# A four-block transformer on one core: local-attention values sent through DRAM, parts of its FFN and table loads moved, and two attentions with their heads' scores put side by side

## The chip, the cores and the metric

The program runs on one core of a Trainium2 chip, in float32. The metric is the device time of one execution in microseconds (us). The engines of a core work side by side, each on its own list of instructions in order, and wait for each other on semaphores: TensorE (PE) multiplies matrices into banks of PSUM; VectorE (DVE), ScalarE (ACT) and GpSimd (POOL) work on rows of 128 partitions; SyncE (SP) issues DMAs.

## What is computed

16 sequences of 256 tokens with 128 channels pass through four blocks, each an attention and a feed-forward part, all with a residual. Block 0 has plain attention (16 heads of 64), block 1 the same with a causal mask, and the second part of block 2 is a stack of six local transformer layers, the largest part of the time:

```python
# block 0 and 1, per sequence and head (block 1: causal mask)
probs = softmax(einsum('bid,bjd->bij', q, k) * 64**-0.5, axis=2)
out = einsum('bij,bjd->bid', probs, v)

# block 2, six times, over 16 heads of 64, windows of 32 tokens
def shift_tokens(t):                   # half of the channels come one token late
    a, s = split(t, 2, -1)
    s = pad(s, ((0, 0), (1, 0), (0, 0)))[:, :-1]
    return concatenate([a, s], -1)

def attn_layer(x, Wqkv, qs, ksc, Wo):
    q, k, v = split(x @ Wqkv, 3, -1)   # into heads
    q, k = l2norm(q) * qs, l2norm(k) * ksc
    q, k = rotary(q), rotary(k)
    # a window's queries look at its own keys and the window's before
    sim = where(mask, -max, einsum('bhwie,bhwje->bhwij', bq, look(bk)) * 8.0)
    out = einsum('bhwij,bhwje->bhwie', softmax(sim, -1), look(bv))
    return out @ Wo

def ffn_layer(x, g, bln, W1, b1, W2, b2):
    xn = layernorm(x) * g + bln
    a, gate = split(xn @ W1 + b1, 2, -1)
    return a * gelu(gate) @ W2 + b2
```

In each local layer both parts get token-shifted input and are added to the residual.

## The kernel before

The kernel writes out, by hand, a list of instructions for each engine and the semaphores between them. No scheduler reorders it: what stands first on an engine runs first.

**`attention`** serves blocks 0 (its names begin with `a0`) and 1 (`a1`). Two heads of 64 are one group; 8 groups of 16 sequences are 128 items. In an item TensorE turns (transposes) the probabilities of an earlier item (`turn`, L494), makes the scores of the next (`scores`, L486), multiplies turned probabilities with values (`weigh`, L505 and L506), projects queries, keys and values for a later one (L465, L472) and projects the output (L514). DVE takes the maximum of the scores (L716; L713 with the mask) and scales the exponentials (L722, L726); ACT makes the exponentials (L605), and copies out of PSUM (L568, L569, L575, L593, L611). The queries and keys of head 0 lie in partitions 0 to 63, of head 1 in 64 to 127. With `by_turns`, which holds for two heads without rotation, the order is turn of head 0, scores of head 0, turn of head 1, scores of head 1.

**`local_layers`** goes through 96 iterations `g`, 6 layers of 16 sequences. An iteration has two halves, `o` = 0 and 1, of 8 heads each; `h = 2g + o` counts halves. A half works on what three steps of the pipeline need: it projects queries and keys for half `h + 2` (`project_rows`, L1019), takes scores of half `h` from 128 small matmuls (`scores`, L1049), projects values (`project_v`, L1025), turns and weighs the probabilities (`turn_probs` L1061, `turn_qk` L1035, `weigh` L1075). DVE rotates queries and keys (L1297, L1301), masks scores and takes their maxima (`shift_scores`, L1330, L1334), sums exponentials (`invert_sums`, L1339, L1341); POOL subtracts the maximum (L951), divides by the sum (L957) and works on the rotation (L937, L944); ACT squares (L1198), copies and makes the exponentials (L1214).

The values of a half are needed in windows of 64 keys (a window and the one before), so each row is needed twice. Before, `x` has a pad of one window, POOL's `copy_window` (L970) writes the transposed input in overlapping windows into `x_windows`, and `project_v` projects each row twice (four matmuls of 512 columns, written as eight passes), with four moves of ACT (`move_v`, L1202).

The output projection (`output`, L1088) of an iteration adds to the residual the attention of the one before (`add_output`). The feed-forward part of an earlier sequence goes along: its rows are normalised (`row_stats` L1348 to L1353, `normalise_rows`), turned (`turn_normed`, L1095), multiplied with two matrices (`gates` and `ups`), the gates pass through Gelu on ACT (`open_gates`, L1237), DVE multiplies both (`hide_rows`, L1371), and TensorE projects down (`give`); DVE adds a bias and that result to the residual (`add_ffn`, L1384, L1388). Half of a row's channels comes one token late: SP brings the shifted rows (`shift`, L881 and L882; 127 partitions, and one row more) and stages the next input (`stage_x`, L876). ACT loads a table (ACT_TABLE_LOAD) when it goes from some functions to others: in the trace a load stands in front of an iteration's first squares (L1198) and one in front of the Gelu (L1237). Behind the Gelu it calls Square on one element (`warm`, L1281).

Where a step waits is written in its function: `output` and `give` wait for `g_freed`, `hide_rows` for `g_filled`, `weigh` for turned probabilities.

Of the kernel before, what the change touches and what calls it, by code (L numbers as in the profile page):

```python
# [286 lines left out]
def attention(core, name, w_dram, src_t, res, groups, heads, causal=False, window=False, scale=None,  # L287
# [39 lines left out]
    with ExitStack() as ctx:  # L327
# [50 lines left out]
        with nc.Block() as block:  # L378
# [64 lines left out]
            def _(pe):  # L443
# [87 lines left out]
                by_turns = heads == 2 and not rotary  # L531

                def item(quad, p, buffers, b, gp):
# [248 lines left out]
def local_layers(core, name, t, y, base, w, fw, gains):  # L782
# [13 lines left out]

    t_filled = core.sems(name, "t_filled0", "t_filled1")
    t_freed = core.sems(name, "t_freed0", "t_freed1")
    (cleared, staged, x_moved, window_ready, f_filled, f_freed, g_filled, g_freed, rows_filled, squared, sin_done, reduced,
     summed, newton, rot_ready) = core.sems(  # L800
        name, "cleared", "staged", "x_moved", "window_ready", "f_filled", "f_freed", "g_filled", "g_freed", "rows_filled",
# [6 lines left out]
     fw_loaded, scales_loaded, tables_ready) = core.sems(  # L808
        name, "shift_loaded", "stats_done", "stats_ready", "var_ready", "rstd_ready", "normed", "bias_added",
        "ffn_added", "w_loaded", "fw_loaded", "scales_loaded", "tables_ready")  # L810

    with ExitStack() as ctx:
# [4 lines left out]
        x, x_windows = sb("x", [P, W + SEQ]), sb("x_windows", [P, 4, 2, 2, W])  # L817
# [27 lines left out]
        def t_fill(h):  # L845

            return 5 * h + 4
# [5 lines left out]
        def hidden_fill(g):  # L853

            return f_fill(g) + (2 if not isinstance(g, int) or g < LAST else 1)
# [16 lines left out]
        with nc.Block() as block:  # L872
            @block.sync
            def _(sp):
# [14 lines left out]
                def iteration(g):  # L889
# [4 lines left out]
                    stage_x(g + 2)  # L894
                    sp.wait_ge(normed, g + 1)
# [3 lines left out]
                    shift((g + NB - 1) & (NB - 1))  # L899

                def load_layer(L):

                    sp.wait_ge(ffn_added, NB * L + 19)
                    sp.sem_inc(begun, 1)
                    sp.dma_start(fw[:], t["f2"][bass.ds(L + 1, 1), :, :].rearrange("a p n -> p (a n)")).then_inc(fw_loaded, DMA)
# [7 lines left out]

                load_scales(0)
                stage_x(0)
                shift(NB - 2)
                sp.wait_ge(f_filled, 1)
                stage_x(1)
                with sp.Fori(0, DEPTH) as L:
                    with sp.Fori(0, 3) as m:  # L920
                        iteration(NB * L + m)
                    load_layer(L)
# [10 lines left out]
            def _(pool):  # L933
# [47 lines left out]
                def iteration(g, last=False):  # L981
                    for o in range(2):
# [5 lines left out]
                        if o == 0:  # L988
                            deviations(g)
# [1502 lines left out]
```

## Time and profile before

| | before |
|---|---|
| median of 3 runs | 7244.83 us (7240.41 to 7246.15) |
| profiled execution | 7247.5 us |
| its span | 7245.8 us |
| mean granted TensorE clock | 0.977 |
| PE busy | 6522.4 us (90%) |
| DVE busy | 4927.7 us (68%) |
| ACT busy | 4182.4 us (58%) |
| POOL busy | 2901.3 us (40%) |

The span is the time from the profile's first to its last record. The busy time of an engine is a sum over stages which differ. The plain attention of block 0 lies between 74 and 857 us, that of block 1 between 1081 and 1765, the local layers between 2241 and 6346.

### The profile page before, as it was taken

How to read it: one execution, taken by the hardware profiler on the slowest of the kernel's cores; microseconds unless marked ns; L12 is line 12 of the kernel's file. 1: busy time of each engine (PE TensorE's matmuls, PEld its weight loads, DVE VectorE, ACT ScalarE, POOL GpSimd, SP SyncE). 2: the span in 40 equal slices, each digit the busy share in tenths (PEclk: the TensorE clock that was granted, in tenths of full speed). 3: DMA queues.
4: the chain of work that ended last, by engine and by line, in shares of the span. 5: the costliest groups of instructions: out<-in, count | busy, mean ns of one | idle time of the engine just before them, and what ended most of it. 6: DMA issues, size and time to landing. Idle time of an engine off the chain costs nothing. (4 is left out here: it accounts for less than half of the span.)

```text
span 7245.8 us, 217809 instructions
## 1 busy us (share of the span) xinstructions
PE 6522.4 (90%) x79314; PEld 4468.9 (62%) x79314; DVE 4927.7 (68%) x14182; ACT 4182.4 (58%) x10030; POOL 2901.3 (40%) x2911
## 2 busy tenths in 40 slices
PE   7999979999988888888888888888888888879998
PEld 5777657776655565555555556555555555557676
DVE  4555535555657777777777777777777777668378
ACT  4666637776224655656655665565665566446355
POOL 0000010000004666666666666666666666530030
PEclk9999989999989999999999999999999999979999
DMA  1000000000000000000000000000000000010210
GB/s 34 24 25 25 23 27 29 28 28 22 10 33 20 23 4 5 23 4 5 5 23 5 4 5 22 5 5 4 23 5 4 23 4 5 5 37 16 81 38 24
DMA packets 131939, 133.17 MB, mean 18 GB/s; under 512 B 40302, under 2 KB 121982, under 8 KB 130814
## 3 DMA queue, kind: packets, MB, share of 16 engines
q1 hardware_dynamic: 115454, 103.45, 4.4%
q0 software_dynamic: 7936, 24.28, 1.1%
q10 hardware_dynamic: 8448, 4.20, 0.2%
q8 instruction: 51, 0.84, 0.0%
q14 instruction: 50, 0.41, 0.0%
HBM read 55.48 MB, written 10.49 MB: 9 GB/s over the span
## 5 line engine op out<-in xcount | busy, mean ns | idle before, releaser
L937 POOL TENSOR_TENSOR l_rot<-l_rot,l_by_sin 128x512 f32<-128x512 f32 x768 | 961.1, 1272 | 438.6 <-DVE l_by_sin L1301 424.5
L944 POOL TENSOR_TENSOR l_rot<-l_rot,l_norms 128x512 f32<-128x512 f32 x768 | 793.7, 1064 | 485.0 <-DVE l_norms L1322 485.0
L1019 PE MATMUL bank<-w_w,l_x 128*128 (+1 forms) x1536 | 802.0, 631 | 133.8 <-DVE l_by_sin L1301 126.3
L1198 ACT ACTIVATE l_squares<-bank 128x512 f32<-128x512 f32 x768 | 447.5, 596 | 518.9 <-DVE l_square_sums L1306 491.8
L1025 PE MATMUL bank<-w_w,l_x_windows 128*128 (+1 forms) x1536 | 721.0, 602 | 0.0
L1297 DVE TENSOR_TENSOR l_rot<-bank,l_cos 128x512 f32<-128x512 f32 x768 | 519.2, 676 | 295.7 <-ACT l_squares L1198 294.4
L486 PE MATMUL bank<-a_qk 64*128 64x256 f32 (+2 forms) x2660 | 679.5, 381 | 6.1 <-DVE a_qk L668 3.5
L402 POOL DMA_DIRECT2D a_w<-in_a x23 | 13.0, 565 | 1554.2 <-PE bank L514 1431.0
L593 ACT ACTIVATE a_probs_t<-bank 128x512 f32<-128x512 f32 (+1 forms) x656 | 355.9, 554 | 353.7 <-PE bank L494 353.7
L1219 ACT ACTIVATE l_probs_t<-bank 128x512 f32<-128x512 f32 x384 | 208.7, 595 | 598.2 <-PE bank L1061 598.2
L1035 PE MATMUL bank<-ident,l_rot 128*128 128x128 f32 x3072 | 476.4, 283 | 74.3 <-ACT l_probs_t L1219 48.0
L1025 PEld LDWEIGHTS bank<-w_w,l_x_windows 128*128 128x128 f32 x1536 | 260.0, 189 | 429.1 <-issue 429.0
L1301 DVE TENSOR_TENSOR l_by_sin<-bank,l_sin 128x512 f32<-128x512 f32 x768 | 521.8, 679 | 0.9 <-POOL l_rot L937 0.9
L1019 PEld LDWEIGHTS bank<-w_w,l_x 128*128 128x128 f32 x1536 | 246.0, 189 | 443.9 <-issue 438.7
L951 POOL TENSOR_TENSOR l_probs<-l_probs,l_best 128x512 f32<-128x512 f32 x384 | 400.2, 1042 | 282.4 <-DVE l_best L1334 282.4
L1202 ACT ACTIVATE l_v<-bank 128x512 f32<-128x512 f32 x768 | 451.3, 588 | 103.6 <-PE bank L1025 103.6
L1208 ACT ACTIVATE l_qk<-bank 128x512 f32<-128x512 f32 x768 | 450.0, 597 | 90.5 <-PE bank L1035 87.2
L486 PEld LDWEIGHTS bank<-a_qk 64*128 64x128 f32 (+1 forms) x2660 | 410.6, 188 | 135.2 <-issue 91.7
L1306 DVE TENSOR_REDUCE l_square_sums<-l_squares 128x8 f32<-128x512 f32 x768 | 486.4, 674 | 0.0
L716 DVE TENSOR_REDUCE a_neg_max<-bank 128x1 f32<-128x256 f32 x780 | 294.6, 419 | 270.8 <-PE bank L486 262.5
L1035 PEld LDWEIGHTS bank<-ident,l_rot 128*128 128x128 f32 x3072 | 322.2, 140 | 229.4 <-ACT l_probs_t L1219 92.7
L957 POOL TENSOR_TENSOR l_probs<-l_probs,l_inverse 128x512 f32<-128x512 f32 x384 | 400.2, 1042 | 126.6 <-DVE l_inverse L1341 126.5
(265 smaller groups left out, 14415.8 us busy)
## 6 DMA issues: line engine op xcount, KB each, us to landing
a_x<-normed_t SPq DMA_DIRECT2D x320, 128.0 KB, 2.0
l_stage_rows<-inner SPq DMA_DIRECT2D x98, 128.0 KB, 2.1
w_w<-in_w SPq DMA_DIRECT2D x6, 2048.0 KB, 9.5
l_shifted_half<-inner SPq DMA_DIRECT2D x98, 63.5 KB
f_w<-in_f SPq DMA_DIRECT2D x9, 514.5 KB, 3.2
a_w<-in_a POOLq DMA_DIRECT2D x18, 256.0 KB, 2.9
f_w<-in_f POOLq DMA_DIRECT2D x9, 512.0 KB, 4.4
c_x<-normed_t SPq DMA_DIRECT2D x36, 128.0 KB, 2.0
```

The lines of the kernel that those rows point to most:

```text
L486: last = nc.tensor.matmul(bank[:, t * SEQ + k0:t * SEQ + k1], queries, qk[p % 2][rows_of_head, keys_at + k0:keys_at + k1], start=True, sto ...
L937: nc.gpsimd.tensor_tensor(rot[s][n][:], rot[s][n][:], by_sin[n % 2][:], ALU.add).then_inc(summed, 1)
L944: nc.gpsimd.tensor_tensor(mine, mine, along(norms[s][:, 8 * n:8 * n + 8], HD), ALU.mult)\
L1019: nc.tensor.matmul(rows_p[i][:], x[:, W + i * P:W + (i + 1) * P], layer_w(layer, quad * QUAD, QUAD), start=True, stop=True).then_inc(rows_ ...
L1025: nc.tensor.matmul(t_p[j % 2][:], x_windows[:, j].rearrange("p t s c -> p (t s c)"), layer_w(layer, wv_at + o * QUAD, QUAD), start=True, s ...
L1035: last = nc.tensor.transpose(t_p[i][:, tile_of(n)], rot[s][2 * a + i][:, tile_of(n)], core.ident[:])
L1198: nc.scalar.activation(squares[i][:], rows_p[i][:], ACT.Square).then_inc(squared, 1)
L1202: nc.scalar.activation(v[:, j, o * QUAD:(o + 1) * QUAD], t_p[j % 2][:], ACT.Copy).then_inc(t_freed[j % 2], 1)
L1208: nc.scalar.activation(qk[o][:, :, 2 * a:2 * a + 2, W + i * P:W + (i + 1) * P], t_p[i][:].rearrange("p (n h s) -> p n h s", n=2, h=2), ACT ...
L1297: nc.vector.tensor_tensor(rot[s][2 * a + i][:], rows_p[i][:], cos[:, i, :], ALU.mult)
L1301: nc.vector.tensor_tensor(dst, src[:, :, ::-1, :], table, ALU.mult).then_inc(sin_done, 1)
L1306: nc.vector.tensor_reduce(square_sums[:, 8 * n:8 * n + 8], squares[i][:].rearrange("p (h d) -> p h d", d=HD), AX, ALU.add)\
```

## The change

In **`attention`** `by_turns` goes. TensorE turns both heads, then makes the scores of both, then weighs.

In **`local_layers`**:

- `x` has no pad, and `x_windows` and `copy_window` go. `project_v` projects each row once, two matmuls for a half in place of four; two moves of ACT put them in `v_rows`. SP stores them to DRAM (`store_v`, 512 KB), behind a window of zeros, and after the weighing of half `h` loads them back into `v` for half `h + 2` as overlapping windows (`load_v`, four DMAs of 256 KB). `weigh` waits for `v_loaded`.
- The FFN: `ups` comes ahead of the scores of the first half and `give` ahead of the scores of the second. On DVE `normalise_rows` begins the iteration, `hide_rows` follows the masked scores of the first half, `add_ffn` and `row_stats` of the next iteration follow those of the second, and `add_output` ends the first half. `fw` is loaded in parts (`gates_loaded`, `ups_loaded`).
- ACT calls Exp on one element (`warm`) at the start of an iteration, and Gelu on one element behind the exponentials of the second half. The first square of an iteration goes to the end of the one before.
- On SP, an iteration is: `stage_x`, the store and the loads of values of the first half, the wait for `normed` and `added`, the `shift`, then the store and the loads of values of the second half.

```diff
@@ attention, item
-                            if by_turns:
-                                scores(k + 1, p + 1, j)
-                        if not by_turns:
-                            for j in pass_heads:
-                                scores(k + 1, p + 1, j)
+                        for j in pass_heads:
+                            scores(k + 1, p + 1, j)
@@ local_layers, SP
+                def store_v(u, o, fill):
...
+                    sp.dma_start(v_dram[o][W:, :].rearrange("(i p) n -> p i n", p=P), v_rows[:]).then_inc(v_stored, DMA)
+                def load_v(u, o):
+                    sp.wait_ge(v_stored, (u + 1) * DMA)
...
+                    for i in range(2):
+                        for s in range(2):
+                            at = i * P + s * W
+                            sp.dma_start(v[HD * i + W * s:HD * i + W * (s + 1), :, o * QUAD:(o + 1) * QUAD],
+                                         v_dram[o][at:at + P, :].rearrange("(j c) n -> c j n", c=W)).then_inc(v_loaded[o], DMA)
+                def send_v(g, o):
+                    h = 2 * g + o
+                    sp.wait_ge(v_loaded[o], (g + 1) * 4 * DMA)
...
+                    store_v(h + 2, o, t_fill(h))
+                    sp.wait_ge(heads_filled, 4 * h + 4)
...
+                    load_v(h + 2, o)
                 def iteration(g, L=None, last=False):
...
                     stage_x(g + 2)
...
+                    if not last:
+                        send_v(g, 0)
                     sp.wait_ge(normed, g + 1)
                     sp.wait_ge(added, g + 2)
                     shift((g + NB - 1) & (NB - 1))
...
+                    if not last:
+                        send_v(g, 1)
@@ PE
                 def project_v(o, fill, layer):
-                    for j in range(4):
...
-                        nc.tensor.matmul(t_p[j % 2][:], x_windows[:, j].rearrange("p t s c -> p (t s c)"),
+                    for i in range(2):
+                        reached(pe, t_freed[i], fill)
+                        nc.tensor.matmul(t_p[i][:], x[:, tile_of(i)], layer_w(layer, wv_at + o * QUAD, QUAD), start=True,
+                                         stop=True).then_inc(t_filled[i], 2)
@@ weigh
+                    pe.wait_ge(v_loaded[o], ((h >> 1) + 1) * 4 * DMA)
@@ iteration, PE
                             project_rows(h + 2, o, 0, (g + 1) >> 4)
+                        if o == 0:
+                            ups(g)
+                        else:
+                            give(g)
                         scores(h, o)
                         if not last:
                             project_rows(h + 2, o, 1, (g + 1) >> 4)
+                            project_v(o, fill, (g + 1) >> 4)
                         if o == 0:
-                            project_v(1, fill, g >> 4)
                             output(g)
-                            give(g)
...
                         weigh(h, o, turned)
-                        if o == 1:
-                            ups(g)
@@ iteration, ACT
+                    nc.scalar.activation(warm[:], core.ones[:, 0:1], ACT.Exp)
...
+                            exps(h, 1)
+                            nc.scalar.activation(warm[:], core.ones[:, 0:1], ACT.Gelu)
                         move_probs(turned)
...
-                            nc.scalar.activation(warm[:], core.ones[:, 0:1], ACT.Square)
                         move_heads(h, o)
+                    if not last and squared_next:
+                        square(2 * g + 4, 0)
@@ iteration, DVE
+                    normalise_rows(g)
...
                         shift_scores(h, 0)
                         shift_scores(h, 1)
+                        if o == 0:
+                            hide_rows(g)
+                        else:
+                            add_ffn(g)
+                            row_stats(g + 1)
                         invert_sums(h, 0)
                         invert_sums(h, 1)
-                        if o == 0:
-                            row_stats(g)
...
                         if o == 0:
                             add_output(g)
-                            add_ffn(g)
-                        else:
-                            hide_rows(g)
```

TensorE, the beginning of an item in block 0's attention, before; `a_probs_0` and `a_probs_1` are the two heads (the rows name instructions of the program, not times):

```order
L494 MATMUL bank<-ident,a_probs_0 128x128 x4
L478 REGISTER_ALU
L480 ISA
L486 MATMUL bank<-a_qk 128x256 x2
L492 REGISTER_ALU
L494 MATMUL bank<-ident,a_probs_1 128x128 x4
L486 MATMUL bank<-a_qk 128x256 x2
L505 MATMUL bank<-a_probs_t,a_v 64x256
L506 MATMUL bank<-a_probs_t,a_v 64x256
L505 MATMUL bank<-a_probs_t,a_v 64x256
L506 MATMUL bank<-a_probs_t,a_v 64x256
```

and after the change:

```order
L494 MATMUL bank<-ident,a_probs_0 128x128 x4
L492 REGISTER_ALU
L494 MATMUL bank<-ident,a_probs_1 128x128 x4
L478 REGISTER_ALU
L480 ISA
L486 MATMUL bank<-a_qk 128x256 x4
L505 MATMUL bank<-a_probs_t,a_v 64x256
L506 MATMUL bank<-a_probs_t,a_v 64x256
L505 MATMUL bank<-a_probs_t,a_v 64x256
L506 MATMUL bank<-a_probs_t,a_v 64x256
```

The scores of both heads now stand next to each other, behind both turns.

TensorE, the second half of a local iteration, from its scores to the values, before:

```order
L1049 MATMUL bank<-l_qk 32x64 x64
L843 REGISTER_ALU
L1019 ISA
L1019 MATMUL bank<-w_w,l_x 128x512
L843 REGISTER_ALU
L1019 MATMUL bank<-w_w,l_x 128x512
L1025 ISA
L1025 MATMUL bank<-w_w,l_x_windows 128x512 x2
L843 REGISTER_ALU
L1025 MATMUL bank<-w_w,l_x_windows 128x512 x2
```

and now, from its first row projection on; `w_f, l_hidden` is `give`, and L1066, L1072 and L1095 are the former L1019, L1025 and L1049:

```order
L1066 MATMUL bank<-w_w,l_x 128x512 x2
L1174 MATMUL bank<-w_f,l_hidden 128x128 x6
L1088 ISA
L1095 MATMUL bank<-l_qk 32x64 x64
L841 REGISTER_ALU
L1066 ISA
L1066 MATMUL bank<-w_w,l_x 128x512
L841 REGISTER_ALU
L1066 MATMUL bank<-w_w,l_x 128x512
L1072 ISA
L1072 MATMUL bank<-w_w,l_x 128x512 x2
```

The down projection came in ahead of the scores, and half of the values' projections are gone.

DVE, the second half of a local iteration, from the first masking to the sums, before:

```order
L1330 TENSOR_TENSOR l_probs<-bank,masks 128x512
L1333 ISA
L1334 TENSOR_REDUCE l_best<-l_probs 128x8
L1330 TENSOR_TENSOR l_probs<-bank,masks 128x512
L1333 REGISTER_ALU
L1334 TENSOR_REDUCE l_best<-l_probs 128x8
L1339 TENSOR_REDUCE l_sums<-l_probs 128x8
L1341 RECIPROCAL l_inverse<-l_sums 128x8
L1339 TENSOR_REDUCE l_sums<-l_probs 128x8
L1341 RECIPROCAL l_inverse<-l_sums 128x8
```

and now, from behind the last maximum (L1405, formerly L1334) to the first sum (L1410, formerly L1339):

```order
L1456 ISA
L1456 TENSOR_TENSOR inner<-inner,w_f 128x256
L1460 TENSOR_TENSOR inner<-inner,bank 128x256
L1416 ISA
L1419 BN_STATS l_stats<-l_shifted_half 128x6
L1420 BN_STATS l_stats<-inner 128x6
L1419 BN_STATS l_stats<-l_shifted_half 128x6
L1420 ISA
L1420 BN_STATS l_stats<-inner 128x6
L1421 ISA
L1424 BN_AGGR l_mean_var<-l_stats 128x2 x2
L1410 TENSOR_REDUCE l_sums<-l_probs 128x8
```

`add_ffn` (L1456, L1460) and the statistics (L1419 to L1424) moved between the maximum and the sum.

## Rows read from the trace of the kernel before

**Rows 1.** Busy time by stretch: us, PE, PEld, DVE, ACT, POOL; PEclk, DMA, GB/s.

```profile
74.00:857.00 783.00, 779.40 (x4560) 558.10 (x4561) 420.69 (x1394) 535.37 (x1778) 4.30 (x8) 1.00 0.07 24
1081.00:1765.00 684.00, 679.94 (x4372) 497.78 (x4370) 388.64 (x2192) 506.72 (x1807) 4.29 (x8) 0.99 0.08 28
2247.00:6307.00 4060.00, 3595.54 (x62587) 2366.20 (x62587) 3082.48 (x7497) 2433.98 (x4318) 2704.27 (x2688) 1.00 0.03 10
```

**Rows 2.** Timeline, first attention: start us, us, engine, line, operation, idle before.

```profile
500.85 0.38 ACT L611 ACTIVATE a_heads_t<-bank 128x256 f32<-128x256 f32 x1 [0.59 <-PE bank L506]
501.13 0.47 ACT L605 ACTIVATE a_probs<-bank,a_neg_max 128x256 f32<-128x256 f32 x1
...
502.02 0.39 ACT L568 ACTIVATE a_qk<-bank 128x256 f32<-128x256 f32 x1
...
502.37 0.62 DVE L726 TENSOR_SCALAR a_probs<-a_probs,a_inverse 128x256 f32<-128x256 f32 x2
...
504.17 0.66 PE L494 MATMUL bank<-ident,a_probs 128*128 128x128 f32 x4
...
504.75 1.13 PE L486 MATMUL bank<-a_qk 64*128 64x256 f32 x4
...
505.92 0.76 DVE L716 TENSOR_REDUCE a_neg_max<-bank 128x1 f32<-128x256 f32 x2 [0.89 <-PE bank L486]
```

**Rows 3.** Timeline of the second attention, same columns.

```profile
1502.71 0.55 PE L494 MATMUL bank<-ident,a_probs 128*128 128x128 f32 x3
...
1503.18 0.92 PE L486 MATMUL bank<-a_qk 64*128 64x128 f32 x4
...
1504.70 0.08 DVE L713 DVE_READ_ACCUMULATOR2_ANT a_neg_max<- 128x1 f32 x1
```

**Rows 4.** Timeline of one iteration of the local layers, same columns.

```profile
4000.34 1.98 PE L1019 MATMUL bank<-w_w,l_x 128*128 x4
...
4002.25 1.48 PE L1049 MATMUL bank<-l_qk 64*32 64x64 f32 x128
...
4010.63 3.73 PE L1088 MATMUL bank<-w_w,l_heads_t 128*128 x32
...
4015.55 1.04 PE L1061 MATMUL bank<-ident,l_probs 128*128 128x128 f32 x8
...
4021.59 1.98 PE L1019 MATMUL bank<-w_w,l_x 128*128 x4
...
4022.77 2.65 SPq L882 DMA_DIRECT2D l_shifted_half<-inner  x1
...
4029.08 0.69 DVE L1334 TENSOR_REDUCE l_best<-l_probs 128x8 f32<-128x512 f32 x1
...
4030.27 0.69 DVE L1339 TENSOR_REDUCE l_sums<-l_probs 128x8 f32<-128x512 f32 x1 [0.50 <-ACT l_probs L1214]
...
4032.59 1.04 POOL L957 TENSOR_TENSOR l_probs<-l_probs,l_inverse 128x512 f32<-128x512 f32 x1 [0.28 <-DVE l_inverse L1341]
...
4042.07 1.27 DVE L1371 SCALAR_TENSOR_TENSOR l_hidden<-bank,w_f,l_gate 128x256 f32<-128x256 f32 x3 [3.50 <-PE bank L1102]
...
4042.45 1.98 PE L1019 MATMUL bank<-w_w,l_x 128*128 x4
```

**Rows 5.** Timeline at the end of the local layers, same columns.

```profile
6317.98 0.42 DVE L1384 TENSOR_TENSOR inner<-inner,w_f 128x256 f32<-128x256 f32 x1
...
6319.50 0.28 DVE L1353 BATCH_NORM_AGGREGATE l_mean_var<-l_stats 128x2 f32<-128x12 f32 x2
...
6321.88 0.75 SPq L881 DMA_DIRECT2D l_shifted_half<-inner  x1
...
6331.82 0.22 DVE L1348 BATCH_NORM_STATS2 l_stats<-l_shifted_half 128x6 f32<-128x64 f32 x1
```

**Rows 6.** DMA issues: queue, count, KB each, median us from issue to landing.

```profile
l_stage_rows<-inner SPq DMA_DIRECT2D x98, 128.0 KB, 2.1
w_w<-in_w SPq DMA_DIRECT2D x6, 2048.0 KB, 9.5
```

More of the change, by code:

```diff
@@ L912, in load_layer, with layer @@
                         .then_inc(w_loaded, DMA)
+                def layer(L):
+                    with sp.Fori(0, 2) as m:
+                        iteration(NB * L + m)
+                    iteration(NB * L + 2, L)
+                    load_layer(L)
                 load_scales(0)
                 stage_x(0)
+                sp.wait_ge(cleared, 2)
+                for o in range(2):
+                    sp.dma_start(v_dram[o][0:W, :], heads_t[0:W, 0:2, :].rearrange("p a n -> p (a n)")).then_inc(v_cleared, DMA)
+                sp.wait_ge(v_cleared, 2 * DMA)
                 shift(NB - 2)
@@ L918, in _ @@
                 stage_x(1)
[L919 to L922, printed above, removed]
+                for u in range(2):
+                    store_v(u, u, u)
+                    load_v(u, u)
+                with sp.Fori(0, DEPTH - 1) as L:
+                    layer(L)
                     with sp.Fori(3, NB) as m:
                         iteration(NB * L + m)
+                layer(DEPTH - 1)
+                with sp.Fori(NB * (DEPTH - 1) + 3, LAST) as g:
+                    iteration(g)
+                iteration(LAST, last=True)
                 sp.wait_ge(normed, LAST + 2)
@@ L1144, in iteration @@
                         fill, more = t_fill(h), o == 0 or not last
-                        turned = fill + 2 if more else fill
+                        turned = fill if last else fill + 1
                         if not last:
@@ L1178, in finish @@
                         gates(g)
-                        ups(g)
+                    ups(LAST + 3)
                     give(LAST + 3)
@@ L1248, in start, with iteration @@
                     square(0, 1)
-                    for j in range(4):
-                        move_v(0, j, 0)
+                    for i in range(2):
+                        move_v(0, i, 0)
                     square(1, 0)
                     square(1, 1)
+                    for i in range(2):
+                        move_v(1, i, 1)
                     move_qk(0, 2)
                     move_x(1, 1)
-                def iteration(g, last=False):
+                def iteration(g, last=False, squared_next=True):
+                    nc.scalar.activation(warm[:], core.ones[:, 0:1], ACT.Exp)
@@ L1257, in iteration @@
                     for o in range(2):
                         h = 2 * g + o
-                        fill, more = t_fill(h), o == 0 or not last
+                        fill = t_fill(h)
+                        turned = fill if last else fill + 1
                         if not last:
-                            square(h + 2, 0)
+                            if o == 1:
+                                square(h + 2, 0)
                             square(h + 2, 1)
-                        if more:
-                            move_v(1 - o, 0, fill)
-                            move_v(1 - o, 1, fill)
@@ L1277, in iteration @@
+                        move_probs(turned)
+                        if o == 0 or not last:
+                            move_qk(1 - o, turned + 1)
                         if o == 0:
@@ L1287, in finish @@
                         open_gates(g)
-                run(act, start, iteration, finish)
+                start()
+                square(2, 0)
+                with act.Fori(0, LAST - 1) as g:
+                    iteration(g)
+                iteration(LAST - 1, squared_next=False)
+                iteration(LAST, last=True)
+                finish()
             @block.vector
```

189 lines of the change are left out of this document (103 added, 86 removed).

## The prediction

> **What bounds the kernel now.** I read the busy time by stretch first. The stretch of the local layers has 4060 us (all but 45 of them), the first attention 783, the second 684 [rows 1], of a span of 7245.8; the change touches these three. In both attentions TensorE is busy over 99% of the stretch, in the local layers 3595.5 of 4060 (89%) with DVE at 76% and POOL at 67%. A busy TensorE need not be the bound: one item of the first attention takes 783/128 = 6.12 us, and to see what its next item waits for I then read the timeline. There the two heads follow each other: transposes of a head's probabilities, the next item's scores of the same head, then the other head; DVE's two maxima start 1.17 us behind the scores [rows 2]. Everything goes round in a loop, with TensorE filling it.
>
> For the local layers I took one iteration of the timeline [rows 4]: 4042.45 − 4000.34 = 42.11 us, in two halves whose projections start at 4000.34 and 4021.59, so 21.25 and 20.86. No engine fills a half. Each half is one chain: project rows, rotate and score, masked maximum (the second of a half ends 4029.08 + 0.69 = 4029.77, 8.18 behind the half's start), subtract and exponentiate, sum (starts 4030.27), divide (the last division ends 4033.63, 3.36 behind the sum), transpose, weigh, then the next half. Transposes to next half: 4015.55 to 4021.59 = 6.04. In the first half the chain is stretched by the values' projection (two of four in each half) and by the FFN, whose gates wait behind table loads; in the second by the up-projection, with `hide_rows` at its very end [rows 4] (its last two rows).
>
> **The attentions, part by part.** Both heads' transposes now come first, then both scores. The contraction of a head is 64 rows, and the two heads sit in different row halves. If they run together, TensorE does 1.13 us less in an item of the first attention. That they can: the 128 score matmuls of 64x32 tiles of the local layers take 1.48 us [rows 4], 11.6 ns each, whereas 4 of 64x128 over 256 columns take 1.13 [rows 2], so 64 columns cost 0.07 and 128 of them 9.0; four quarters of the columns alone would leave 2.3, so row halves overlap too. With less work than the loop is long, what then sets the item is the loop: second transpose to scores 504.75 − 504.17 = 0.58; scores to DVE 505.92 − 504.75 = 1.17; the first head's two maxima 0.76; a wait of 0.10; the first head's exponentials 502.02 − 501.13 = 0.89; the heads' copy between, 501.13 − 500.85 = 0.28; the second head's exponentials to the end of its scaling, 502.37 + 0.62 − 501.13 = 1.86; a wait of 0.06. Sum 5.70 [rows 2]. So 6.11 − 5.70 = 0.41 less, times 128 items: **−52**. The two waits are estimates, the smallest gaps between such neighbours. By TensorE alone it would be −1.13 x 128 = −145; if the heads' scores don't overlap, the maxima come 1.13 later in the loop, 6.8 in place of 6.11, +0.69 x 128 = +88.
>
> The Trainium skill, "TensorEngine Tiling (Array Packing)", section "Theoretical Speedup", gives up to 2x for a contraction of at most 64. By that sentence the whole 1.13 would be won; it speaks of the array, and is the rule behind rival B.
>
> The second attention is causal and its scores are shorter: 0.92 us a head [rows 3]. Its loop: transposes 1502.71 to the end of the maxima 1504.78 = 2.07, then 0.10 + 0.89 + 0.28 + 1.86 + 0.06 as above, 5.26 in all, against 684/128 = 5.34 now: 0.08 x 128 = **−10**. By TensorE alone −0.92 x 128 = −118; without overlap 6.16, +105.
>
> **The local layers, part by part.** (1) Values: the projection falls from 4 matmuls of a half to 2, the moves of ACT likewise, POOL's window copies go; a store of 512 KB and four loads of 256 KB come for each half through DRAM. TensorE loses about what four passes of the row projection take, 1.98 us a half [rows 4], work that is off the chain except where it holds the next waiting instruction. A loaded value is used a whole iteration later: 38 us as summed below, less its issues, against 9.5 us for a 2 MB load [rows 6], so I cost the loads at nothing; they would show from a latency of that length. (2) Table loads: two of an iteration, in front of the squares and of the gates; now ACT makes them where it waits for TensorE. They have no term of their own, since I build the new halves from links that hold none. (3) The FFN: ups ahead of the scores of the first half, `hide_rows` (1.27 [rows 4]) between the maxima and the sums there; give ahead of the scores of the second, `add_ffn` and the statistics between maxima and sums there. From the end of the stage, where nothing else runs, 6317.98 to 6319.50 + 0.28 is 1.80 for the latter [rows 5]; I take 2.0, an estimate, since ACT and POOL run beside it here. Neither hides fully behind ACT's exponentials, which they wait beside: the gap from maximum to sum is only 0.50 [rows 4].
>
> New first half: 8.18 + 1.27 = 9.45; 0.1 wait; the output projection ahead of the transposes holds TensorE about 3.6 (3.73 now [rows 4]), longer than the 3.36 of sums to division: 13.2; then 6.04 to the next half: 19.25. New second half: 8.18 + 2.0 = 10.2; 3.36; 0.1; and 6.04 less an estimated 0.4, since half of its transposes (1.04 for eight [rows 4]) are done before the last division, less 0.3, without the normalised rows' transpose: 5.35: 19.0. Together 38.25 against 42.11, −3.86 in each of 95 repeats: **−367**. Of the bounds: nothing gained if the FFN's 3.07 in the chain replace as much of what they remove (rival D); and TensorE's work, 3595.54/4060 x 42.11 = 37.3 less 2 x 1.98 = 33.3 in an iteration, as the floor, −8.8 x 95 = −836, which the chains above don't let it reach. The clock was granted in full in these stretches (1.00, 0.99, 1.00: 2.4 GHz [rows 1]), with TensorE at 89% in the last; 33.3 of 38.25 is 87%, so I change nothing for it.
>
> (4) The shift of rows, needed by the statistics, is issued by SP after the values' store and loads of the first half. SP waits there for the weighing, about +19.25; four issues at 0.45 to 0.75 (the shift's own first issue [rows 5]; 0.45 is my estimate for them), then the shift's two, 0.75 and 2.65 [rows 4, 5], end at +24.5 to 25.7, and it lands 2.1 later (a 128 KB transfer's [rows 6]): +26.6 to 27.8. The statistics want it behind the maxima and two additions of 0.42 [rows 5]: 19.25 + 8.18 + 0.84 = 28.3. So it is in time by 0.5 to 1.7 us, and I cost it at nothing. The upper end is in the end of the stage: issued from 6321.88, used at 6331.82 [rows 5], 9.9 us; with that it lands 2.8 too late.
>
> The Trainium skill, "DMA: Bandwidth & Descriptors", section "Why a DMA increments its semaphore by 16 and not by 1", says that a transfer of 127 partitions runs on a single DMA engine; the shift has 127 rows, so the megabyte of values issued ahead of it would keep that engine's queue. No row here splits transfers by engine; it speaks for rivals A and A'.
>
> Sum against the profiled execution's 7247.5: −52 − 10 − 367 gives 6818; this execution is 2.7 above the median of the runs, so **6816**.
>
> **Rivals.** *A: the shift is late* by up to the 2.8 us above: at 2 us in each of 95 iterations, +190: 7006; at 2.8, 7082. For it: SP now has five more issues and three waits ahead of the shift. Against: the slack of 0.5 to 1.7 us, if it lands as small transfers do. *A', on the slow side: the shift late behind the megabyte of values.* With 4.7 us of a load ahead of it (half of 9.5 for half the bytes [rows 6]) on top of 2.8, 7.5 late: 6816 + 712 = 7530. It decides from about 4.5 us late, where 95 x 4.5 = 428 eats the gain. Against: the page's DMA share of the stretch is 0.03 [rows 1], so the queues are empty but for this. *B: TensorE stays the bound in both attentions* and the loops overlap better than I add them: −145 − 118 in place of −62: 6615. Against: DVE's wait behind the scores is in the loop. *C: the heads' scores don't overlap*, +88 + 105 in place of −62: 7071. Against: the 1.48 us of the local scores. *D: the local layers stay at 42.1*, because the FFN's links now lie in the chain: 7247.5 − 2.7 − 62 = 7183. For it: DVE goes to 84% busy in the new iteration (32.0 of 38.25) and its queue is in order.
>
> **Numbers.** Forecast 0.62, A 0.15, A' 0.07, B 0.05, C 0.06, D 0.05. The forecast's own range is 6740 to 6900: each half's sum may be off by 0.4 us, which is 76 over 95 iterations. The range that takes in A and C: 6720 to 7082; outside are B, D, A' with 0.17. This kernel's measurement can tell 0.2% from no change. Faster: all but A' and the lateness between A and A', 0.91; same 0.01; slower 0.08.
>
> **What will show it.** The period between two iterations' first projections, 38.25; the halves 19.25 and 19.0; an item of 5.70 in the first attention and 5.26 in the second, with TensorE's share there falling below 95% and DVE named as the releaser of the exponentials. The statistics' first instruction without a wait for a DMA behind the second half's maxima: with such a wait it is A or A', and its length says which. Scores of both heads in one 1.13 us group, else C. No table load with a TensorE wait behind it. I am wrong if the halves are not shortened in the places named: the sum depends on the two links into which the FFN went being 1.27 and 2.0, and on TensorE's 3.6 of output standing beside the division.

## The result, and the profile after

The changed kernel takes 7376.39 us (median of 4 runs, 7374.58 to 7378.20) against 7242.62 before: ratio 1.0184, 95% interval 1.0172 to 1.0197. It is 1.8% slower; I had forecast 6816 us.

| | before | after |
|---|---|---|
| span of the profiled execution | 7245.8 us | 7376.5 us |
| mean granted TensorE clock | 0.977 | 0.947 |
| PE busy | 6522.4 us (90%) | 6135.0 us (83%) |
| DVE busy | 4927.7 us (68%) | 5156.6 us (70%) |
| ACT busy | 4182.4 us (58%) | 3982.4 us (54%) |
| POOL busy | 2901.3 us (40%) | 2823.1 us (38%) |

Busy time by stretch, after, the same stretches and columns as [rows 1] (each kernel is at another place of its work in the last of them):

```profile
74.00:857.00 783.00, 706.09 (x4763) 511.56 (x4764) 441.73 (x1437) 548.20 (x1842) 4.38 (x8) 0.99 0.08 27
1081.00:1765.00 684.00, 611.38 (x4374) 445.96 (x4373) 400.08 (x2159) 471.06 (x1694) 3.76 (x7) 1.00 0.08 27
2247.00:6307.00 4060.00, 3266.68 (x58959) 2343.10 (x58960) 3164.66 (x7157) 2157.45 (x3846) 2505.48 (x2382) 0.95 0.31 80
```

The loss lies in the third row: TensorE's granted clock (the share of its full clock that the chip lets it have), 1.00 before, is 0.95 in the local layers, and DVE is busier although the stretch now holds fewer iterations (92 outputs of 32 passes; before, 96).

The two attentions did what was forecast. Timeline of the first one, with [rows 2] before (start us, us, engine, line, operation):

```profile
505.64 0.66 PE L494 MATMUL bank<-ident,a_probs 128*128 128x128 f32 x4 [0.52 <-DVE a_probs L722]
...
506.22 1.14 PE L486 MATMUL bank<-a_qk 64*128 64x256 f32 x8
...
511.29 0.66 PE L494 MATMUL bank<-ident,a_probs 128*128 128x128 f32 x4 [0.52 <-DVE a_probs L722]
```

Both heads' scores, now eight passes in one group, take 1.14 us; one head's four took 1.13. An item takes 511.29 − 505.64 = 5.65 us (forecast 5.70, before 6.11). In the second attention, with [rows 3] before:

```profile
1502.50 0.55 PE L494 MATMUL bank<-ident,a_probs 128*128 128x128 f32 x3 [0.59 <-DVE a_probs L722]
...
1502.98 0.93 PE L486 MATMUL bank<-a_qk 64*128 64x128 f32 x8
...
1507.58 0.55 PE L494 MATMUL bank<-ident,a_probs 128*128 128x128 f32 x3 [0.58 <-DVE a_probs L722]
```

7.58 − 2.50 = 5.08 us an item (forecast 5.26, before 5.34).

Now one iteration of the local layers, with [rows 4] before; L1066 is the row projection (L1019), L1135 the output (L1088), L1432 `normalise_rows`, L1419 the first of the statistics:

```profile
4010.36 1.98 PE L1066 MATMUL bank<-w_w,l_x 128*128 x4 [0.59 <-issue]
...
4012.12 1.08 DVE L1432 TENSOR_SCALAR l_normed_rows<-inner,l_mean_var,l_rstd 128x64 f32 x1
...
4018.95 0.69 DVE L1405 TENSOR_REDUCE l_best<-l_probs 128x8 f32<-128x512 f32 x1
...
4019.56 1.26 DVE L1443 SCALAR_TENSOR_TENSOR l_hidden<-bank,w_f,l_gate 128x256 f32<-128x256 f32 x3
...
4021.30 5.46 PE L1135 MATMUL bank<-w_w,l_heads_t 128*128 x32 [2.52 <-DVE l_hidden L1443]
...
4026.59 1.04 PE L1107 MATMUL bank<-ident,l_probs 128*128 128x128 f32 x8
...
4032.64 1.98 PE L1066 MATMUL bank<-w_w,l_x 128*128 x4
...
4035.30 0.78 SPq L887 DMA_DIRECT2D l_shifted_half<-inner  x1
...
4036.22 4.76 SPq L888 DMA_DIRECT2D l_shifted_half<-inner  x1
...
4043.57 0.23 DVE L1419 BATCH_NORM_STATS2 l_stats<-l_shifted_half 128x6 f32<-128x64 f32 x1 [1.96 <-DMA l_shifted_half<-inner]
...
4044.53 0.63 DVE L1410 TENSOR_REDUCE l_sums<-l_probs 128x8 f32<-128x512 f32 x1
```

and the projection that begins the next iteration:

```profile
4053.66 1.55 PE L1066 MATMUL bank<-w_w,l_x 128*128 x3 [0.62 <-issue]
```

The first half takes 4032.64 − 4010.36 = 22.28 us in place of the forecast 19.25, the second 4053.66 − 4032.64 = 21.02 in place of 19.0: 43.3 against 42.11 before. The mean is longer, 4060/92 = 44.1 us in the stretch of the local layers. Three things stand in these lines that the forecast didn't have: normalisations of 1.08 us at the start, an output projection of 5.46 us in place of 3.73, and 1.96 us in which DVE waits for the shift's DMA before the statistics.

The clock of TensorE in this iteration (us, busy time of PE, PEld, DVE, ACT, POOL, then PEclk, DMA share and GB/s):

```profile
4018.80:4021.30 2.50, 0.00 (x1) 0.01 (x1) 2.46 (x6) 1.62 (x3) 1.68 (x2) 1.00 0.00 0
4021.30:4023.00 1.70, 1.70 (x8) 1.70 (x9) 1.63 (x6) 0.61 (x2) 1.28 (x2) 0.52 0.05 17
4023.00:4025.00 2.00, 2.00 (x12) 2.00 (x12) 2.00 (x5) 0.00 (x0) 2.00 (x3) 0.56 0.66 248
4025.00:4026.80 1.80, 1.80 (x18) 1.80 (x18) 1.66 (x6) 0.00 (x0) 1.22 (x1) 1.00 0.00 0
4032.64:4053.66 21.02, 15.69 (x319) 10.81 (x313) 16.05 (x39) 12.82 (x24) 10.44 (x11) 1.00 0.31 78
```

TensorE waits 2.5 us for `hide_rows`; then, in the output, the granted clock is 0.52 and 0.56, the lower of its two levels (1.2 GHz in place of 2.4), and 1.00 again at the output's end. Over the whole run the output's passes are busy for 507.2 us, before the change for 364.2.

Groups of DVE's instructions in the stretch of the local layers (busy us, mean ns, idle time before and its releaser):

```profile
L1432 DVE TENSOR_SCALAR l_normed_rows<-inner,l_mean_var,l_rstd 128x64 f32 (+1 forms) x182 | 187.9, 1033 | 86.1 <-DVE l_norms L1393 79.1 <-issue 5.8 <-DVE l_sin L1465 1.0
L1432 DVE TENSOR_SCALAR l_normed_rows<-l_shifted_half,l_mean_var,l_rstd 128x64 f32<-128x64 f32 x182 | 135.1, 742 | 0.0
...
L1419 DVE BATCH_NORM_STATS2 l_stats<-l_shifted_half 128x6 f32<-128x64 f32 x184 | 40.1, 218 | 204.8 <-DMA l_shifted_half<-inner 204.8
```

The normalisations' means are 1033 and 742 ns; the statistics wait 204.8 us for the shift, 2.2 us an iteration.

### The profile page after: what moved, and what is told of

It reads as the page before. It is cut to its first block and busy times, and to the rows that moved or that the text cites. A ratio compares the mean times of both kernels' runs of the same rounds, so it can differ in the third digit from the quotient of the medians.

```text
span 7376.5 us, 217475 instructions
## 1 busy us (share of the span) xinstructions
PE 6135.0 (83%) x78552; PEld 4414.5 (60%) x78552; DVE 5156.6 (70%) x14186; ACT 3982.4 (54%) x9742; POOL 2823.1 (38%) x2719
## 5 line engine op out<-in xcount | busy, mean ns | idle before, releaser
L1066 PE MATMUL bank<-w_w,l_x 128*128 (+1 forms) x1536 | 784.8, 628 | 115.4 <-issue 57.4
L1135 PE MATMUL bank<-w_w,l_heads_t 128*128 (+1 forms) x3104 | 507.2, 340 | 236.4 <-DVE l_hidden L1443 236.4
L1135 PEld LDWEIGHTS bank<-w_w,l_heads_t 128*128 128x128 f32 x3104 | 489.2, 252 | 315.4 <-issue 315.4
L1081 PE MATMUL bank<-ident,l_rot 128*128 128x128 f32 x3072 | 513.0, 305 | 79.8 <-ACT l_probs_t L1272 46.2
L601 ACT ACTIVATE a_probs<-bank,a_neg_max 128x256 f32<-128x256 f32 x780 | 363.1, 476 | 271.1 <-DVE a_neg_max L712 271.1
L494 PE MATMUL bank<-ident,a_probs 128*128 128x128 f32 x2352 | 374.1, 282 | 148.8 <-DVE a_probs L722 148.8
L1081 PEld LDWEIGHTS bank<-ident,l_rot 128*128 128x128 f32 x3072 | 368.9, 154 | 206.8 <-issue 95.3
L1066 PEld LDWEIGHTS bank<-w_w,l_x 128*128 128x128 f32 x1536 | 254.8, 190 | 370.2 <-issue 364.9
L486 PE MATMUL bank<-a_qk 64*128 64x256 f32 (+2 forms) x2660 | 423.7, 383 | 4.4 <-DVE a_qk L664 3.5
## 6 DMA issues: line engine op xcount, KB each, us to landing
l_shifted_half<-inner SPq DMA_DIRECT2D x98, 63.5 KB
```

Of the source, the lines that this page charges most:

```text
L486: last = nc.tensor.matmul(bank[:, t * SEQ + k0:t * SEQ + k1], queries, qk[p % 2][rows_of_head, keys_at + k0:keys_at + k1], start=True, sto ...
L1066: nc.tensor.matmul(rows_p[i][:], x[:, tile_of(i)], layer_w(layer, quad * QUAD, QUAD), start=True, stop=True).then_inc(rows_filled, 1)
L1081: last = nc.tensor.transpose(t_p[i][:, tile_of(n)], rot[s][2 * a + i][:, tile_of(n)], core.ident[:])
L1135: last = nc.tensor.matmul(out_p[:, tile_of(i)], heads_t[:, pair, tile_of(i)], layer_w(layer, wo_at + pair * P, P), start=pair == 0, stop=p ...
```

## The experiments

Each time stands beside one of the kernel before from the same chip, as a ratio with its 95% interval. The first four runs change one thing of the changed kernel each.

**The shift ahead of the loads.** SP's iteration:

```diff
-    send_v(g, 0)             # store, wait for the weighing, load
+    save_v(g, 0)             # store
     sp.wait_ge(normed, g + 1)
     sp.wait_ge(added, g + 2)
     shift((g + NB - 1) & (NB - 1))
+    fetch_v(g, 0)            # wait for the weighing, load
```

> In the first half SP issues the shift of rows before it waits for the weighing and loads the values; all else as in the changed kernel. Theory (the shift is late because it comes behind the loads of values): the statistics no longer wait for a DMA (204.8 us of that wait in the stretch of the local layers, about 2.2 an iteration); the sums that follow wait next for ACT's second exponentials, so about 1.5 us of an iteration are won: 96 x 1.5 = 144 less than 7376, about 7232. Rival (the statistics are not on the chain, TensorE's output and its clock set the iteration): the wait goes and the time stays within 30 us of 7376.

Measured 7077.39 us (ratio to before 0.9773, 0.9757 to 0.9790): 299 less than the changed kernel, twice what the wait alone was to give. DVE's groups:

```profile
L1438 DVE TENSOR_SCALAR l_normed_rows<-inner,l_mean_var,l_rstd 128x64 f32 (+1 forms) x186 | 190.8, 1026 | 87.8 <-DVE l_norms L1399 80.8 <-issue 5.8 <-DVE l_sin L1471 1.2
...
L1425 DVE BATCH_NORM_STATS2 l_stats<-l_shifted_half 128x6 f32<-128x64 f32 x188 | 40.3, 214 | 0.0
```

No wait is left before the statistics (L1425), and the normalisations are as slow as ever. TensorE's clock changed as well. An output (first row) and the second half of an iteration:

```profile
4014.66:4018.30 3.64, 3.64 (x32) 3.64 (x33) 3.57 (x9) 0.61 (x2) 3.22 (x3) 1.00 0.38 144
4024.38:4043.55 19.17, 15.57 (x319) 10.78 (x313) 15.89 (x39) 12.85 (x25) 12.13 (x13) 1.00 0.33 85
```

Before this output, too, TensorE idled 2.52 us, yet it runs at 1.00. What differs is the second half, in which TensorE now idles 19.17 − 15.57 = 3.60 us; in the changed kernel, 21.02 − 15.69 = 5.33 us. In the stretch of the local layers an output (32 passes) takes 396.2/93.8 = 4.22 us in the mean here, 480.1/92 = 5.22 there, 96 x 1.0 less. This output is not all of them: of the run's 97, 26 still take over 4.4 us, in the changed kernel 84. The transposes of the rotated queries and keys (L1081 in the changed kernel) are busy for 457.9 us in place of 513.0 over the run. With the 205 of the wait these parts come to 356, more than the 299, so not all of them lie on the chain.

**The shift in two pieces.** SP's order as changed; 127 partitions become 112 and 15, and the statistics wait for one transfer more:

```diff
-    sp.dma_start(shifted_half[1:P], rows[0:P - 1])
+    sp.dma_start(shifted_half[1:113], rows[0:112])
+    sp.dma_start(shifted_half[113:P], rows[112:P - 1])
...
-    dve.wait_ge(shift_loaded, (g + 1) * 2 * DMA)
+    dve.wait_ge(shift_loaded, (g + 1) * 3 * DMA)
```

> Order of SP as in the changed kernel; only the shift's transfer of 127 partitions is issued as one of 112 and one of 15. Theory (the transfer of 127 partitions runs at 15 GB/s, as the trace shows behind the loads, because one DMA engine does it alone): the pieces land some 3 us sooner and the statistics don't wait: about 7232, as with the shift put first. Rival (it is late because it is issued late, or queues behind the loads whatever its shape): the wait shrinks by less than 0.5 us of 2.2, and the time by less than 40 us.

Measured 7072.09 us (0.9764, 0.9748 to 0.9781), the same as with the order changed. To see why, the DMA rate in the changed kernel, 40 slices of 0.4 us from 4030 us on:

```profile
DMA  0000000000889999999995100000010199930000
GB/s 0 0 0 0 0 0 0 0 0 0 164 307 353 225 195 179 241 282 215 210 179 89 10 15 16 15 15 16 15 16 16 47 379 374 389 133 0 0 0 0
```

The loads of values run at up to 353 GB/s from slice 10 on (counted from 0). When they are done, some 3.6 us follow (slices 22 to 30) at 15 to 16 GB/s, the first at 10, with under a tenth of the engines busy: I read that as the shift. Its 63.5 KB at this rate are 4.1 us. In the split kernel, slices of 0.4 us from 4021 us on, the two pieces with the us from issue to landing, and DVE's group:

```profile
GB/s 0 0 0 0 0 0 0 0 0 0 0 0 0 0 0 0 0 0 0 0 0 0 236 276 302 261 195 184 225 230 205 200 205 163 97 6 0 0 0 0
...
l_shifted_half<-inner SPq DMA_DIRECT2D x1, 56.0 KB, 4.6
l_shifted_half<-inner SPq DMA_DIRECT2D x1, 7.5 KB, 4.0
```

```profile
L1420 DVE BATCH_NORM_STATS2 l_stats<-l_shifted_half 128x6 f32<-128x64 f32 x188 | 40.3, 214 | 0.0
```

The slow tail is gone and the statistics don't wait. So the shape of the transfer made it late, not its place behind the loads alone: either change is enough. The Trainium skill, "DMA: Bandwidth & Descriptors", section "Why a DMA increments its semaphore by 16 and not by 1", states that a transfer of 127 partitions runs on one engine; by its rule for the number of engines one of 112 runs on sixteen. The 15 to 16 GB/s and their end in the split agree, though no row here splits transfers by engine.

**The normalisation at its old place.**

```diff
-    normalise_rows(g)        # DVE, start of the iteration
     for o in range(2):
...
             sum_squares(h + 2, 1)
+        if o == 0:
+            normalise_rows(g)
+        if not last:
             norm_factors(h + 2, o)
```

> DVE normalises the rows where the kernel before did, behind the second sums of squares of the first half, not at the start of the iteration. Theory (the four normalisations, 0.74 to 1.03 us each now and 0.36 to 0.38 before, hold up the rotation by 1.1 us at the start of an iteration while POOL works): the first maxima come 1.1 sooner after the half's projection, TensorE idles less before its output: 96 x 1.1 = 105 less at least, 7270, and down to 7130 if the clock no longer falls in the output. Rival (the instructions are slow wherever they stand, and come to the chain at the new place): mean durations stay over 0.7, time within 30 us of 7376.

Measured 7073.05 us (0.9766, 0.9749 to 0.9782), 303 less. DVE's groups, and an output of this kernel:

```profile
L1432 DVE TENSOR_SCALAR l_normed_rows<-inner,l_mean_var,l_rstd 128x64 f32 (+1 forms) x188 | 63.2, 336 | 0.0
L1432 DVE TENSOR_SCALAR l_normed_rows<-l_shifted_half,l_mean_var,l_rstd 128x64 f32<-128x64 f32 x188 | 56.9, 303 | 0.0
L1419 DVE BATCH_NORM_STATS2 l_stats<-l_shifted_half 128x6 f32<-128x64 f32 x188 | 41.0, 218 | 214.1 <-DMA l_shifted_half<-inner 214.1
```

```profile
4013.20 3.83 PE L1135 MATMUL bank<-w_w,l_heads_t 128*128 x32 [1.45 <-DVE l_hidden L1443]
```

The same instructions take 336 and 303 ns at the other place, TensorE waits 1.45 us in place of 2.52 before the output, and the output takes 3.83 (5 of the run's 97 take over 4.4). The wait for the shift (L1419) stays, 214.1 us, and the second half stays long.

**More work for TensorE.** In the first half each matmul of the values is made twice:

```diff
+    if twice:
+        nc.tensor.matmul(t_p[i][:], x[:, tile_of(i)], layer_w(...), start=True, stop=True)
     nc.tensor.matmul(t_p[i][:], x[:, tile_of(i)], layer_w(...), start=True, stop=True).then_inc(...)
```

> In the first half each matmul of the values is done twice (the same result), 1.9 us more work for TensorE in the time in which it idles 2.4 us for the hidden rows before its output. Theory (the clock falls to half behind that idle time, and makes the output 5.5 us in place of 3.7): with the idle time filled the output takes 3.7 again, and the kernel with more work is faster by up to 96 x 1.55 = 149, about 7230 to 7290. Rival (the clock falls for another reason, or the added work delays the chain): the output stays at 5.5 and the time is 7376 or longer, by up to 96 x 1.9 = 182.

Measured 7249.57 us (1.0010, 1.0001 to 1.0020): 127 less than the changed kernel, with more work. The last of the doubled projections, the output, and the transposes of the rotated queries and keys (L1084) in the second half of the same iteration:

```profile
4010.10 1.02 PE L1075 MATMUL bank<-w_w,l_x 128*128 x2
4011.93 3.83 PE L1138 MATMUL bank<-w_w,l_heads_t 128*128 x32 [0.80 <-DVE l_hidden L1446]
...
4037.32 3.74 PE L1084 MATMUL bank<-ident,l_rot 128*128 128x128 f32 x16
```

The idle time before the output is 0.80 us, and it takes 3.83; only one of the run's 97 outputs takes over 4.4. So the fall of the clock in the output comes from TensorE's idling, and without it the kernel is 127 us shorter, the added work included. But the clock still falls elsewhere: in the second half, where nothing was filled, the transposes take 3.74 us at a granted clock of 0.54 (the same sixteen passes take 2.62 in the first half), and the stretch of the local layers has 0.97, against 0.95 in the changed kernel. So the 127 us are not the price of the whole fall.

**Both orders together.** The edits of the first and the third experiment.

> Both orders together: SP issues the shift before it loads the values, and DVE normalises where the kernel before did. Theory (two separate delays, one in each half, each of which also let the clock fall in TensorE's output): the first half takes 19.56 as with the late normalisation alone, the second 19.17 as with the early shift alone, 38.7 us an iteration: about 7073 - 96 x 2.0 = 6880. Rival (each of the two changes alone had already won what there is, namely the clock, and a third link takes over): 7040 or more.

Measured 6850.83 us (0.9463, 0.9448 to 0.9479): 5.4% faster than before, 526 less than the changed kernel. Alone the two won 299 + 303 = 602, so 76 are counted twice, as is to be expected if each alone had already won back much of the clock. The local layers' row of the stretches, and an iteration:

```profile
2247.00:5900.00 3653.00, 3136.26 (x60725) 2231.55 (x60717) 2998.77 (x7320) 2204.09 (x3945) 2568.11 (x2440) 1.00 0.35 91
```

```profile
4091.96 1.98 PE L1072 MATMUL bank<-w_w,l_x 128*128 x4 [0.64 <-issue]
...
4101.79 3.83 PE L1141 MATMUL bank<-w_w,l_heads_t 128*128 x32 [1.42 <-DVE l_hidden L1449]
...
4111.51 1.98 PE L1072 MATMUL bank<-w_w,l_x 128*128 x4
...
4130.60 1.98 PE L1072 MATMUL bank<-w_w,l_x 128*128 x4 [0.59 <-issue]
```

The clock is 1.00, and 4 of the run's 97 outputs take over 4.4 us. The halves take 4111.51 − 4091.96 = 19.55 and 4130.60 − 4111.51 = 19.09 us, 38.64 together: the forecast had 19.25 and 19.0.

**Without the early table loads**, from the run with both orders:

```diff
-    nc.scalar.activation(warm[:], core.ones[:, 0:1], ACT.Exp)
...
-            nc.scalar.activation(warm[:], core.ones[:, 0:1], ACT.Gelu)
```

> As the run with both orders, without the two calls of ACT on one element that load the tables early. Theory (a table load in front of the first half's exponentials is on the chain, that in front of the Gelu beside TensorE's weighing): 96 x 1.28 = 123 more than with them, and 246 if both are on the chain. Rival (ACT waits there anyway, the loads hide): within 20 us of the run with both orders.

Measured 6871.57 us (0.9489, 0.9473 to 0.9505): 21 more, not the 123 to 246 of the theory. ACT's groups:

```profile
L1296 ACT ACT_TABLE_LOAD x94 | 120.6, 1283 | 1.7
L1255 ACT ACT_TABLE_LOAD x92 | 118.0, 1283 | 308.4 <-PE bank L1072 308.4
```

Both loads, 1283 ns each, are there in every iteration, one in front of the Gelu (L1296) and one of the squares (L1255). So the chain bears 21/96 = 0.2 us of their 2.57 us; the two calls are worth little. That doesn't hold for the place of the loads: this run keeps the first squares at the end of the iteration before, and the load of L1255 comes where ACT has waited for TensorE, 308.4 us in all. In the kernel before, it stood in front of the first squares:

```profile
4001.56 1.28 ACT L1198 ACT_TABLE_LOAD   x1 [1.39 <-PE bank L1019]
...
4003.48 0.69 DVE L1297 TENSOR_TENSOR l_rot<-bank,l_cos 128x512 f32<-128x512 f32 x1 [2.26 <-ACT l_squares L1198]
...
4023.46 0.69 DVE L1297 TENSOR_TENSOR l_rot<-bank,l_cos 128x512 f32<-128x512 f32 x1 [0.92 <-ACT l_squares L1198]
```

There the rotation begins 4003.48 − 4000.34 = 3.14 us behind the projection [rows 4], in the second half, without a load, 4023.46 − 4021.59 = 1.87. So that load lengthened the way to the rotation by 1.27 us. No run moves the squares back alone.

**The attentions alone**, in the kernel before:

```diff
-    by_turns = heads == 2 and not rotary
+    by_turns = False
```

> The kernel before with the one change to the two attentions: both heads turned, then both scored. Theory (the part is independent of the rest, an item of the first attention 5.65 in place of 6.11, of the second near 5.26): 128 x 0.46 + 128 x 0.08 = 69 less than before, about 7174. Rival (the gain in the attentions is given back in the stages that follow): within 0.2% of before.

Measured 7159.66 us (0.9884, 0.9868 to 0.9901), 83 less than before; I had 62 in the prediction. The items' 0.46 and 0.26 us by 128 give 92. So the part is independent of the rest, and worth a third more than I had added up.

**The normalisation in another form**, at the changed place:

```diff
-    tensor_scalar(normed_rows[...], rows, mean_var[:, i, 0:1], rstd[:, i:i + 1], ALU.subtract, ALU.mult)
+    scalar_tensor_tensor(normed_rows[...], rows, mean_var[:, i, 0:1], rstd[:, i:i + 1].to_broadcast([P, D // 2]), ALU.subtract, ALU.mult)
```

> As the changed kernel, the four normalisations at the start of an iteration, but each as a SCALAR_TENSOR_TENSOR with the factor as a second tensor of SBUF (broadcast over the row) in place of a TENSOR_SCALAR with two factors. Theory (a DVE instruction of this size is held up only in the TENSOR_SCALAR form, by POOL's instruction that runs beside it): 0.2 to 0.4 us each in place of 0.74 to 1.03, and the time falls as with the late normalisation, to 7073 or near. Rival 1 (with two operands from SBUF the other form is held up by POOL just as well, as the Trainium skill's page on SBUF has it for two-input instructions): 0.7 us or more each, time within 30 us of 7376. Rival 2 (it is the place at the start of the iteration, whatever the instructions last): they are short, and the time stays.

Measured 7380.72 us (1.0186, 1.0168 to 1.0204): rival 1. The timeline of POOL's four multiplications with the norms, and DVE's instructions beside them:

```profile
4012.77 4.12 POOL L1005 TENSOR_TENSOR l_rot<-l_rot,l_norms 128x512 f32<-128x512 f32 x4 [2.37 <-DVE l_norms L1393]
...
4013.70 0.28 DVE L1432 SCALAR_TENSOR_TENSOR l_normed_rows<-inner,l_mean_var,l_rstd 128x64 f32<-128x64 f32 x1 [1.01 <-DVE l_norms L1393]
4013.90 1.06 DVE L1432 SCALAR_TENSOR_TENSOR l_normed_rows<-l_shifted_half,l_mean_var,l_rstd 128x64 f32<-128x64 f32 x1
...
4014.89 1.08 DVE L1432 SCALAR_TENSOR_TENSOR l_normed_rows<-inner,l_mean_var,l_rstd 128x64 f32<-128x64 f32 x1
```

One takes 0.28 us; the ones that follow take 1.06 and 1.08, the length of one of POOL's four (4.12/4 = 1.03), and each ends as one of POOL's ends. In the run with the late normalisation POOL idles there, and they take 0.30 to 0.38. The Trainium skill, "SBUF — State Buffer", section "Who interferes with whom", states it as a shared pair of ports: a DVE instruction with two inputs from SBUF contends with a GpSimd instruction that reads SBUF, and so does one in a mode that uses both ports, which `tensor_scalar` can enter, and there the later of the two is blocked for the whole of the other's instruction. The lengths in both forms agree; which mode the `tensor_scalar` ran in, no row shows.

## Why the prediction was wrong

**The attentions: right.** The heads overlap, and the loop became the bound: 5.65 for 5.70, 5.08 for 5.26. Rivals B and C fall. The second attention's loop, summed with the first one's terms, came out 0.18 us too long, so the two together won 83 us alone where I had 62.

**The lengths of the halves: right, once nothing else is late.** 19.55 and 19.09 against 19.25 and 19.0 in the run with both orders; that run's 6850.83 is 0.5% from the forecast. In the first half each link is within 0.3 us of its term (second maximum 8.17 behind the projection, for 8.18; output 9.83, for 9.55). In the second there is some luck: the sums start at 9.83, for 10.2, and the rest takes 9.26, for 8.8. Rival D falls too: the FFN's links don't cost what they remove.

**The shift: the step that failed by its size.** I let it land 2.1 us after its issue, as a 128 KB transfer does, "in time by 0.5 to 1.7 us", and took the 9.9 us of the stage's end for a bound only. It takes some 4 us by itself at 15 GB/s, behind the loads, and the statistics began 4043.57 − 4010.36 = 33.2 us into the iteration shown, where I had them at 28.3; 3.0 of the difference is the longer first half. The wait is 2.2 us an iteration, which is rival A's size (2 us, priced at 190); undoing it won 299, with the clock's part in it.

**The normalisation: a move that I didn't price.** This term I left out. The prediction listed `hide_rows`, `add_ffn` and the statistics as what moves on DVE, not `normalise_rows`, which now opens the iteration, beside POOL's multiplications with the norms; undoing it won 303, with the clock's part in it. The first half's maxima end 4018.95 + 0.69 − 4010.36 = 9.28 behind its projection, where I had 8.18.

**The clock: "I change nothing for it".** I took TensorE's busy share of the whole stretch, 87%, for the answer. The two delays add idle time in both halves, the share fell to 80% (3266.68 of 4060), and the output behind the wait ran at the lower level: 5.46 in place of 3.73 us, where my sum had 3.6. Against the run with both orders the outputs are busy for 507.2 − 379.4 = 128 us more and the transposes of the rotated queries and keys for 513.0 − 457.9 = 55 more, so the clock costs some 180 us of TensorE's time, an estimate; how much of it lies on the chain was not isolated. The filled idle time gave back 127.

In the iteration shown: output starts 4021.30 − 4010.36 = 10.94 behind the projection (forecast 9.55: +1.39, of it 1.10 by the normalisation); output to transposes 5.29 (3.6: +1.69, nearly all the clock: 5.46 in place of 3.83); transposes to the second half 6.05 (6.04). In the second half the sum starts at 11.89 (10.2: +1.69, the shift), the rest is +0.3. Together +5.1 of 43.3 − 38.25.

**The range and the rivals.** Rival A had the size of the wait, and A' its place behind the values, at 7.5 us; neither had the shift's own slow rate. By A's price the wait alone would have left a gain, and the run with the late normalisation, which keeps the wait, is faster than before. It turned into a loss because the normalisation and the clock came with it, and no rival had two of them together: the range ended at 7082.

**Table loads: right to give them no term.** The first half was built from the second's 8.18, which holds no load, and measures 8.17 with both orders. The two calls that load them early add 21 us to that, not more.

What stays open: why the clock falls in one iteration and not in the next. With the same idle time of some 2.5 us before it, an output was slow in 84 of 97 iterations of the changed kernel and in 26 with the shift first; with 1.45 us in 5, and with 0.80 in one, though there the clock still fell in the second half.

## What to carry to other kernels

Price every instruction that a change moves, by what runs beside it at the new place, not by its duration at the old one: an instruction of some 0.36 us took 1.08 beside POOL. When a DMA gets a new place in a queue, read its own duration from its bytes and rate, and look how its rows are cut, since 112 and 15 landed in time where 127 did not. And where several small delays leave TensorE idle, look at its granted clock before adding them up: undone one by one the two delays here won 299 and 303 us, together 526. And look at the clock of the whole stretch, not of one group: with the idle time filled in one place it still fell in another.

## What the runs showed of the hardware

- TensorE with more work was faster: 7249.57 against 7376.39 us, since the output behind 0.80 us of idle time in place of 2.52 ran at 2.4 GHz, not 1.2; in the second half the clock still fell, to 0.54 in the transposes.
- A transfer of 127 partitions moved at 15 to 16 GB/s, where the loads of values moved at up to 353.
- DVE's 64-column instructions took 0.30 to 0.38 us with POOL idle and 1.06 to 1.18 us beside POOL's multiplications, in two forms, and the profile counts the longer time as busy, not as waiting.
